# A normalised, attention-mixed 1x1 convolution with residual: eviction on VectorE, low halves and bias on GpSimd

## What is computed

```python
xg = _gn(x)                                   # group norm, 32 groups
pooled = jnp.mean(xg, axis=(2, 3))
h = relu((pooled @ fc_w.T - abn_m) * (abn_g / sqrt(abn_v + EPS)) + abn_b)
ch_att = sigmoid(h @ ch_w.T + ch_b)
fl_att = sigmoid(h @ fl_w.T + fl_b)
kn_att = softmax(h @ kn_w.T + kn_b, axis=1)
agg_w = einsum('bk,koc->boc', kn_att, weight)
y = einsum('bchw,boc->bohw', xg * ch_att[:, :, None, None], agg_w)
y = y * fl_att[:, :, None, None]
inv = bn_g / sqrt(bn_v + EPS)
y = (y - bn_m[None, :, None, None]) * inv[None, :, None, None] + bn_b[None, :, None, None]
return x + y
```

## Time and profile before

| | before |
|---|---|
| time, median of 3 runs | 2114.44 us |
| lowest and highest run | 2112.9 and 2115.34 us |
| profiled execution, span from first to last instruction | 2112.4 us |
| mean granted TensorE clock | 0.998 |
| busy PE, DVE, ACT, POOL | 2056.3, 1867.6, 1729.7, 0.2 us |

### The profile page before, as it was taken

The page is one execution under the profiler, slowest core; times in us unless marked ns, Lnnn a source line. Parts: engine busy times, 40 slices in busy tenths (PEclk is TensorE's granted clock), DMA queues, the critical chain, the costliest instruction groups (busy, mean ns, idle before and its releaser), DMA issues.

```text
span 2112.4 us, 33140 instructions
## 1 busy us (share of the span) xinstructions
PE 2056.3 (97%) x10948; PEld 1078.1 (51%) x10948; DVE 1867.6 (88%) x2886; ACT 1729.7 (82%) x2295; POOL 0.2 (0%) x4
## 2 busy tenths in 40 slices
PE   1999999999999999999999999999999999999998
PEld 0455555555555555555555555555555555555554
DVE  7889889889889899889899898898898998898973
ACT  4788888888888888888888888888888888888885
POOL 0000000000000000000000000000000000000000
PEclk9999999999999999999999999999999999999999
DMA  8465556565556565556655565665565655566522
GB/s 332 139 209 194 204 189 206 200 208 203 195 193 208 195 206 202 196 191 208 208 200 200 191 208 193 208 208 191 191 208 202 206 200 192 195 205 207 175 105 105
DMA packets 237284, 415.99 MB, mean 197 GB/s; under 512 B 7248, under 2 KB 236624, under 8 KB 236752
## 3 DMA queue, kind: packets, MB, share of 16 engines
q1 hardware_dynamic: 237264, 415.74, 57.6%
HBM read 210.19 MB, written 205.52 MB: 197 GB/s over the span
## 4 chain that ended last, share of the span: by engine, by line
PE 97%; DVE 1%; DMA 1%; ACT 1%; SPq 0%; issue 0%; DVEq 0%
PE product L679 32%; PE product L680 32%; PE product L681 32%; DMA x_ring<-x 1%; DVE mixed_weight L529 0%; DVE chunk_stats L349 0%; PE small L649 0%; SPq L193 0%; DVE w_lo L545 0%; PE small L640 0%; ACT y L290 0%; PE small L644 0%; ACT x_norm L227 0%; DVE x_lo L357 0%; ACT x_hi L236 0%
## 5 line engine op out<-in xcount | busy, mean ns | idle before, releaser
L679 PE MATMUL product<-x_hi,w_hi 128*128 128x448 f16 x3584 | 1264.5, 353 | 6.7 <-DVE x_lo L357 3.7
L680 PE MATMUL product<-x_lo,w_hi 128*128 128x448 f16 x3584 | 1264.6, 353 | 0.0
L681 PE MATMUL product<-x_hi,w_lo 128*128 128x448 f16 x3584 | 1264.4, 353 | 0.0
L245 ACT ACTIVATE y<-product,out_bias,out_scale 128x448 f32<-128x448 f32 x896 | 641.8, 716 | 275.2 <-PE product L681 270.5
L227 ACT ACTIVATE x_norm<-x_ring,norm_bias,norm_scale 128x448 f32<-128x448 f32 x896 | 671.1, 750 | 1.3 <-DVE norm_bias L409 1.3
L363 DVE TENSOR_TENSOR x_ring<-x_ring,y 128x896 f32<-128x896 f32 x448 | 481.5, 1087 | 100.0 <-ACT y L245 95.7
L679 PEld LDWEIGHTS product<-x_hi,w_hi 128*128 128x128 f16 x3584 | 356.1, 99 | 327.3 <-issue 5.1
L681 PEld LDWEIGHTS product<-x_hi,w_lo 128*128 128x128 f16 x3584 | 350.9, 98 | 328.2 <-issue 1.6
L680 PEld LDWEIGHTS product<-x_lo,w_hi 128*128 128x128 f16 x3584 | 350.8, 98 | 319.5 <-issue 1.3
L349 DVE BATCH_NORM_STATS2 chunk_stats<-x_ring 128x6 f32<-128x448 f32 x896 | 493.4, 616 | 1.3 <-DMA x_ring<-x 1.2
L357 DVE TENSOR_TENSOR x_lo<-x_norm,x_hi 128x1792 f16<-128x1792 f32 x224 | 452.4, 2019 | 19.7 <-ACT x_hi L236 19.7
(11 more groups left out here) (66 smaller groups left out, 261.5 us busy)
## 6 DMA issues: line engine op xcount, KB each, us to landing
x_ring<-x SPq DMA_DIRECT2D x224, 896.0 KB, 4.8
out<-x_ring SPq DMA_DIRECT2D x224, 896.0 KB, 3.9
weight<-wt SPq DMA_DIRECT2D x4, 1024.0 KB, 15.1
params<-par SPq DMA_DIRECT2D x1, 462.0 KB, 3.4
```

The lines of the kernel that those rows point to most:

```text
L245: nc.scalar.activation(y[:, s % 2, t], acc[k % BANKS][:, 0:COLS], ACT.Identity, bias=obias[:, t:t + 1], scale=oscale[:, u, t:t + 1]).then_ ...
L679: nc.tensor.matmul(bank, whi[:, u, t, cols], hi, start=(t == 0), stop=False)
L680: nc.tensor.matmul(bank, whi[:, u, t, cols], lo, start=False, stop=False)
L681: ins = nc.tensor.matmul(bank, wlo[:, u, t, cols], hi, start=False, stop=(t == CT - 1))
```

## The change

ScalarE no longer evicts. VectorE's new `evacuate` is one scalar_tensor_tensor a tile: it reads the bank, multiplies by the output scale and adds the ring slot in place, once `mm_done` and `biased` have come. The output bias is put into the ring slot before, by GpSimd (`add_bias`, four operations of 448 columns a chunk), after GpSimd has made the chunk's low half (`split`, now a tensor_tensor on GpSimd). The buffer `y` is gone, with its waits; the weights' absolute sums get a scratch buffer. ScalarE's `split` now waits for `mm_done` of the chunk that used the buffer before (the count starts at 4). SP waits for `evac_done` instead of `add_done`.

```diff
-        y = sb("y", [P, 2, CT, COLS])
+        scratch = sb("abs_scratch", [P, CT * C])
...
@@ -204,7 +203,7 @@
-                    sp.wait_ge(add_done, turn.at(2 * RING, 4 + 2 * (s + 1)))
+                    sp.wait_ge(evac_done, turn.at(4 * RING, BANKS + 4 * (s + 1)))
...
@@ -229,21 +228,13 @@
-            def split(turn, f):
+            def split(turn, f, first=False):
 
 
                 act.wait_ge(xn_ready, turn.at(RING, f + 1))
+                if not first:
+                    act.wait_ge(mm_done, turn.at(4 * RING, 4 * f))
                 nc.scalar.activation(xhi[:, f % 2], xn[:, f % 2], ACT.Copy).then_inc(hi_ready, 1)
-
-            def evacuate(turn, s, t):
-
-                k = 4 * s + t
-                u = s // CHUNKS
-                act.wait_ge(mm_done, turn.at(4 * RING, k + 1))
-                if t % 2 == 0:
-                    act.wait_ge(add_done, turn.at(2 * RING, 2 * s + t // 2 + 1))
-                nc.scalar.activation(y[:, s % 2, t], acc[k % BANKS][:, 0:COLS], ACT.Identity,
-                                     bias=obias[:, t:t + 1], scale=oscale[:, u, t:t + 1]).then_inc(evac_done, 1)
...
@@ -311,7 +301,6 @@
-                        evacuate(turn, s, t)
...
@@ -350,17 +339,14 @@
-            def split(turn, f):
-
-
-                dve.wait_ge(hi_ready, turn.at(RING, f + 1))
-                nc.vector.tensor_tensor(xlo[:, f % 2], xn[:, f % 2], xhi[:, f % 2], ALU.subtract).then_inc(lo_ready, 1)
-
-            def add(turn, s, half):
-
-                dve.wait_ge(evac_done, turn.at(4 * RING, BANKS + 4 * s + 2 * half + 2))
-                two = slice(2 * half, 2 * half + 2)
-                nc.vector.tensor_tensor(xs[:, s, two], xs[:, s, two], y[:, s % 2, two], ALU.add).then_inc(add_done, 1)
+            def evacuate(turn, s, t):
+
+                k = 4 * s + t
+                dve.wait_ge(mm_done, turn.at(4 * RING, 4 + k + 1))
+                dve.wait_ge(biased, turn.at(4 * RING, k + 1))
+                nc.vector.scalar_tensor_tensor(out=xs[:, s, t], in0=acc[k % BANKS][:, 0:COLS],
+                                               scalar=oscale[:, s // CHUNKS, t:t + 1], in1=xs[:, s, t],
+                                               op0=ALU.mult, op1=ALU.add).then_inc(evac_done, 1)
...
@@ -513,7 +499,6 @@
-            split(start, 0)
...
@@ -595,10 +580,6 @@
-                        if t == 0 and s:
-                            if prepare and n == 2:
-                                stats_complete(turn, b)
-                            add(turn, s - 1, 1)
...
-                        if t == 1 and not (last and s + SPLIT_AHEAD >= RING):
-                            split(turn, s + SPLIT_AHEAD)
-                        if t == 2:
-                            add(turn, s, 0)
...
@@ -625,13 +602,45 @@
+                        if prepare and (n, t) == (1, 3):
+                            stats_complete(turn, b)
+                        evacuate(turn, s, t)
...
-                add(turn, RING - 1, 1)
...
+        @block.gpsimd
+        def _(pool):
+            def split(turn, f):
+
+
+                pool.wait_ge(hi_ready, turn.at(RING, f + 1))
+                nc.gpsimd.tensor_tensor(xlo[:, f % 2], xn[:, f % 2], xhi[:, f % 2], ALU.subtract).then_inc(lo_ready, 1)
+
+            def add_bias(f):
+
+
+                for t in range(CT):
+                    nc.gpsimd.tensor_scalar(xs[:, f % RING, t], xs[:, f % RING, t], obias[:, t:t + 1], None,
+                                            ALU.add).then_inc(biased, 1)
+
+            start = Turn(pool, 0)
+            pool.wait_ge(obias_ready, 1)
+            split(start, 0)
+            add_bias(0)
+
+            def body(i, last):
+                turn = Turn(pool, i)
+                for s in range(RING):
+                    if not (last and s + SPLIT_AHEAD >= RING):
+                        split(turn, s + SPLIT_AHEAD)
+                        add_bias(s + SPLIT_AHEAD)
...
@@ -650,6 +659,7 @@
+            pe.sem_inc(mm_done, 4)
```

More of the change, by code:

```diff
@@ L134, in build @@
         top_row, top_all = small[0:1, 64:64 + P], small[:, 200:201]
-        y_free = y[:, :, :, :].rearrange("p a t n -> p (a t n)")[:, 0:CT * C]
         def p_(name):
@@ L164, in build @@
         lo_ready = sem("lo_ready")
-        add_done = sem("add_done")
+        obias_ready = sem("obias_ready")
+        biased = sem("biased")
         ln_ready = sem("ln_ready")
@@ L274, in _ @@
             act.preload_act_table_set("natural_log_exp_and_others")
-            act.sem_inc(evac_done, BANKS)
             start = Turn(act, 0)
@@ L283, in _ @@
                 norm(start, 0, t)
-            split(start, 0)
+            split(start, 0, True)
             for k in range(KERNELS):
@@ L289, in _ @@
                     act.wait_ge(abs_done, k)
-                nc.scalar.activation(y_free, w[:, k], ACT.Abs, accum_out=wsum[:, k:k + 1]).then_inc(abs_done, 1)
+                nc.scalar.activation(scratch[:, :].rearrange("p (t n) -> p t n", t=CT), w[:, k], ACT.Abs, accum_out=wsum[:, k:k + 1]).then_inc(abs_done, 1)
                 if k == 0:
@@ L485, in _ @@
             start = Turn(dve, 0)
-            dve.sem_inc(add_done, 4)
+            dve.sem_inc(evac_done, BANKS)
             nc.vector.memset(ones[:, :], 1.0).then_inc(const_ready, 1)
@@ L497, in _ @@
             after(start)
-            step(nc.vector.tensor_tensor(obias[:, :], p_("bn_b"), obias[:, :], ALU.subtract))
+            nc.vector.tensor_tensor(obias[:, :], p_("bn_b"), obias[:, :], ALU.subtract).then_inc(obias_ready, 1)
             for f in range(CHUNKS):
@@ L627, in body @@
                                     split_weight(turn, b, j)
+                        if prepare and (n, t) == (1, 3):
+                            stats_complete(turn, b)
+                        evacuate(turn, s, t)
                     if s == CHUNKS - 1:
                         assert done[0] - before == STEPS, done[0] - before
-                add(turn, RING - 1, 1)
             with dve.Fori(0, TURNS - 1) as i:
+                body(i, False)
+            body(TURNS - 1, True)
+        @block.gpsimd
[17 more added lines that the diff above has]
+                        add_bias(s + SPLIT_AHEAD)
+            with pool.Fori(0, TURNS - 1) as i:
                 body(i, False)
```

## The result

The change takes **2449.32 us** (median of 4 runs, 2443.49 to 2451.26) where the kernel before takes 2114.89: a ratio of 1.1579, with an interval from 1.1562 to 1.1595. I had forecast 2246 us in a range of 2110 to 2460. The direction holds, and so does the first of the two waits; the loss of 334 us is two and a half times the 132 of the forecast. The profiled span is 2441.7 us, 329.3 above the one before.

A forecast was written before the change was run, and what follows sets the result against it. TensorE, busy 97% of 2112.4 us, was taken as the bound. Less 1.1 us of tail, plus 31 x (3.0 + 1.3) = 133 us of waits gives 2244 us; 2 us from span to median make 2246, range 2110 to 2460.

The forecast's parts named there:

- the two waits: TensorE's waits once an image on 31 images: 3.0 us for the norms, 1.3 us around the mixing; 133 us together.
- The clock: TensorE's slow clock after a pause: no loss taken; 1.5 us a pause, 93 us, kept for the upper end.
- Place two: The mixing: GpSimd and VectorE take turns before chunk 6, making its `x_lo` 1.3 us late; ends 0 and 4 us.
- The price of a bias addition: GpSimd's time for one addition of 448 columns: 0.75 us, from a range of 0.55 to 1.5.
- `x_lo` 3.7 us early: GpSimd needs 6.4 us of a chunk's 9.08, so `x_lo` would be ready 5.4 us into it.
- The hold, where I had to choose: VectorE's two-operand operations beside GpSimd: whoever is second waits for the whole instruction; sum 2244 us, chance 0.52.
- Side by side: Rival: GpSimd and VectorE don't block each other, TensorE stays full; 2113 us, from 2111 to 2115, chance 0.31.
- Place one: The norms of an image: GpSimd's work delays VectorE's chain, TensorE waits 3.0 us before the matmul on `fc_pooled`; 0.8 to 8.
- GpSimd alone too slow: Rival: split and four additions pass 9.08 us a chunk, GpSimd sets the pace; 205 us more, 2318 us, chance 0.12.
- The forecast of VectorE's eviction: One VectorE eviction of 448 columns takes 683 ns, at 1.04 ns a column; 896 of them.
- the cover for evictions: A bank must be free only seven tiles after it was filled, some 13 us, so late evictions have cover.
- ScalarE's busy time: ScalarE loses the eviction's 642 us from 1730, leaving 1088 us, so it does not bound.

## Why the prediction had the direction right and the loss too small

In the prediction's own sum the idle time was 31 x (3.0 + 1.3) = 133 us and the clock nothing. Measured, each place costs 3.4 us on 31 images, 211.3 us of added idle time in all, and the busy time grew by 118.0. Three steps failed.

*The clock was set to nothing*, which is the largest miss. The pauses of 2.48 and 3.48 us shown were each followed by a stretch at a granted clock of 0.50. Some of the 118.0 us isn't clock: in the run without additions about 30 pauses without such a stretch raised the busy time by 7.6 us. By that measure some 16 us of the 118 are the pauses' own, and the clock cost about 102, an estimate, more than the 93 that I kept for the upper end.

*Place two had the wrong mechanism.* I forecast `x_lo` of chunk 6 late by 1.3 us through turns between GpSimd and VectorE. It is `x_lo` of the next image's first chunk, late by 3.4 us through ScalarE's queue: 106 us in place of 40. I had costed the third mix as if nobody queued behind it. The run that moves `w_hi` shows it for the kernel with the split alone on GpSimd; in the changed kernel the same move cuts the wait for `x_lo` from 101.7 to 70.9 us and lengthens the other.

*The price of a bias addition was too low.* I took 0.75 us from a range of 0.55 to 1.5; it is 1.39, near the upper end. The split was right (3.4 taken, 3.59 measured). So a chunk is 9.08 us of GpSimd's time and not 6.4, and "`x_lo` 3.7 us early" became no slack at all. 284 us of the loss are gone in the run without additions.

*The hold, where I had to choose, was chosen rightly for two-operand instructions.* "Side by side" is excluded by the run with two-operand work beside the old kernel, where mixes go from 2347 to 3713 ns. The Trainium skill's rule (SBUF — State Buffer, "Who interferes with whom"), that the second is blocked until the first ends, agrees there. It doesn't hold for the one-operand additions: by it the mix at 1002.50 would be held to the end of the addition of 1002.46, 1.37 us, and it was held 0.40. Here the measurement decides. My reason for expecting a hold, that before no second engine read SBUF beside VectorE, was wrong as written: ScalarE's `norm` and `split` read SBUF buffers all the time (1051 us of the earlier trace rows), and the mixes took their 2347 ns beside it. What was absent was GpSimd.

*Place one, 3.0 us forecast*, came to 3.4 (2.48 in the image shown), but by luck in one term. I let four additions slip in at their whole price of 0.75. At the measured price my formula gives 981.1 + 1.95 + 3.59 + 4 x (1.39 + 0.2) + 0.6 = 993.6, so 5.7 us; the additions' short holds, which I did not know of, made up for the price that I had too low.

*GpSimd alone too slow* would by its own formula have cost next to nothing at 9.08 of 9.08, and the run with one long addition shows the same loss at 64% busy. The forecast of VectorE's eviction (683 ns, measured 674) and of the cover for evictions held: VectorE waits for the additions only 7.7 us in all. ScalarE's busy time came to 1141.0 us, not 1088: neighbouring rows of it overlap, so that a group's busy time can't simply be taken off.

What stays open: how the loss divides between sum and holds in the changed kernel itself. Taking GpSimd's additions away removes both at once; making them shorter in sum made them longer each. Nor do the runs tell why a one-operand GpSimd instruction lets go of a two-operand one of VectorE after 0.4 to 0.5 us but held `norm_scale` to its end, nor why the small `kernel_sum` reduction beside memsets took 670 ns instead of 150: it stands right behind a held `TENSOR_SCALAR`.

## What to carry to other kernels

Two-operand work moved to GpSimd can hold a two-operand instruction of VectorE for its whole length, 3.59 us here. That is paid wherever VectorE has a chain of such steps that another engine waits for: list these chains, and what stands behind each waiter in its in-order queue, before moving anything. Ask of each such chain how early it is now; here one was 0.4 us early, and one reordering in a third engine's queue was worth 2.8%. Where the helper's own sum came up to the bound's pace, the same reordering brought back 12 us of 334, and two together 26; the likely reason, which no run isolates, is that nothing lost to a hold can be made up.

## What the hardware showed that I had not expected

- A GpSimd `tensor_scalar` with a per-partition operand over 448 columns takes 1.39 us; a two-operand `tensor_tensor` takes 3.17 to 3.59 over 1792 columns and 2.61 over 1152. From the subtractions of two widths, (3.59 - 2.61) / 640, I estimate 1.5 ns a column and 0.8 us that don't depend on the width; by this estimate four short additions are dear because they are four. No run has both forms at one width. The Trainium skill (GPSIMD Engine Reference, "Elementwise — side-by-side cycle accounting") puts the split at an estimated 3.9 us, near the 3.59 here.
- Between two-operand instructions the hold goes both ways (the split of 1006.49 took 5.65 us, the third mix 5.07). A one-operand addition of 1.40 us holds one of VectorE's in its first 0.4 to 0.5 us only.
- Tiny `TENSOR_SCALAR` instructions with a single SBUF tensor operand are held too: `sigmoids`, 157 ns before, took 1990 ns in the changed kernel, and 716 beside mere memsets.
- The length of a pause alone doesn't tell what it costs in clock. The 62 pauses of the changed kernel, 2.3 to 4.0 us each, added 118.0 / 62 = 1.9 us of busy time each on average, and the one of 2.48 us was followed by half clock. In the run with one long addition this one of 2.73 us was followed by matmuls at their full 0.19 us a step:

```profile
1003.54 0.49 PE L658 MATMUL small<-fc_pooled,ones 128*128 128x128 f32 x2 [2.73 <-DVE fc_pooled L397]
1003.87 0.35 PE L689 MATMUL product<-x_hi,w_hi 128*128 128x448 f16 x1
1004.05 0.35 PE L690 MATMUL product<-x_lo,w_hi 128*128 128x448 f16 x1
```
